# Cross-attention: one accumulated output projection per batch instead of one per step

## The reference, cut to what matters

```python
o = jnp.einsum('bhnm,bhmd->bhnd', a, v)           # a: softmax over 1601 keys
o = o.transpose(0, 2, 1, 3).reshape(xq.shape[0], xq.shape[1], MID)   # MID = 16 * 64
return o @ wo + bo                                # then added to x
```

## Time and profile before

| | us |
|---|---|
| median of 3 runs | 2189.35 (2186.43 to 2197.72) |
| the profiled execution | 2197.43 |
| its span in the trace | 2195.6 |
| PE busy | 2070.3 (94%) |
| DVE busy | 1646.5 (75%) |
| POOL busy | 1169.5 (53%) |
| ACT busy | 998.3 (45%) |
| mean granted TensorE clock | 0.97 of 2.4 GHz |

### The profile page before, as it was taken

One profiled execution on the slowest core, in us unless ns is written; L12 is line 12 of the kernel. 1 busy time (PEld: TensorE's weight loads), 2 busy tenths in 40 slices (PEclk: granted clock), 3 DMA queues, 4 the chain that ended last, 5 costly groups with the idle time before them and its releaser, 6 DMA issues.

```text
span 2195.6 us, 47792 instructions
## 1 busy us (share of the span) xinstructions
PE 2070.3 (94%) x17744; PEld 1412.6 (64%) x17744; DVE 1646.5 (75%) x2426; ACT 998.3 (45%) x1606; POOL 1169.5 (53%) x721
## 2 busy tenths in 40 slices
PE   5888888888699999999999999999999999999988
PEld 3666666622267777777777677777777777777763
DVE  3888888746567877877877787787788778778732
ACT  2444444434244454444444445444444444544433
POOL 1344444300056666666666666666666666666660
PEclk7999999979689999999999999999999999999999
DMA  3522222100111111111111111111111111111100
GB/s 107 161 77 76 76 77 77 53 0 1 41 45 55 49 52 52 52 52 48 52 53 48 55 48 52 52 52 52 48 52 51 49 55 48 52 51 50 51 14 21
DMA packets 109728, 118.32 MB, mean 54 GB/s; under 512 B 18241, under 2 KB 99265, under 8 KB 109249
## 3 DMA queue, kind: packets, MB, share of 16 engines
q1 hardware_dynamic: 109504, 115.27, 15.9%
HBM read 36.52 MB, written 1.05 MB: 17 GB/s over the span
## 4 chain that ended last, share of the span: by engine, by line
PE 89%; DVE 3%; ACT 3%; DMA 3%; issue 2%; SPq 1%; POOL 0%; POOLq 0%; ACTq 0%; DVEq 0%
PE S L1071 20%; PE OB L1083 17%; PE PB L1022 9%; PE PB L1031 9%; PE S L1044 6%; PE S L967 3%; PE OB L977 2%; PE S L879 2%; PE PB L952 2%; PE PB L934 2%; PE PB L1014 2%; PE PB L925 2%; DMA swapped<-turned 2%; PE PB L1092 2%; PE PB L994 1%
## 5 line engine op out<-in xcount | busy, mean ns | idle before, releaser
L502 POOL TENSOR_TENSOR psum_acc<-psum_acc,P 124x1024 f32<-124x1024 f32 (+1 forms) x320 | 688.0, 2150 | 179.8 <-ACT P L627 169.7
L810 DVE TENSOR_REDUCE mxc<-S 128x2 f32<-128x800 f32 (+1 forms) x512 | 507.6, 991 | 230.4 <-PE S L1044 224.9
L627 ACT ACTIVATE P<-S 124x1024 f32<-124x1024 f32 (+1 forms) x448 | 431.4, 963 | 368.3 <-PE S L1071 366.6
L1083 PE MATMUL OB<-P,V 124*64 124x256 f32 (+1 forms) x3328 | 425.7, 387 | 0.0
L495 POOL TENSOR_TENSOR psum_acc<-P 124x1024 f32<-124x1024 f32 x64 | 152.8, 2387 | 348.3 <-ACT P L627 348.3
L519 ACT ACTIVATE V<-PB 124x512 f32<-124x512 f32 (+1 forms) x320 | 157.3, 492 | 330.4 <-PE PB L1031 266.0
L1083 PEld LDWEIGHTS OB<-P,V 124*64 124x64 f32 (+1 forms) x3328 | 220.4, 137 | 115.0 <-issue 15.0
L1071 PE MATMUL S<-QH,KH 64*124 64x256 f32 (+1 forms) x1664 | 268.3, 318 | 4.6 <-ACT P L627 4.6
L1031 PEld LDWEIGHTS PB<-kv_w,ctxT_all 96*124 96x124 f32 (+1 forms) x1664 | 212.3, 188 | 64.0 <-issue 33.0
L1022 PE MATMUL PB<-ctxT_all,kv_w 96*128 96x400 f32 (+1 forms) x512 | 241.4, 554 | 10.9 <-DVE KL L802 7.0
L1031 PE MATMUL PB<-kv_w,ctxT_all 96*124 96x128 f32 (+1 forms) x1664 | 238.8, 282 | 0.1
(11 more groups left out here) (117 smaller groups left out, 3146.7 us busy)
## 6 DMA issues: line engine op xcount, KB each, us to landing
swapped<-turned SPq DMA_DIRECT2D x384, 100.0 KB, 2.0
swapped<-turned SPq DMA_DIRECT2D x128, 128.0 KB, 2.0
swapped<-turned SPq DMA_DIRECT2D x128, 100.2 KB, 2.0
kv_w<-sa_kv_dram SPq DMA_DIRECT2D x64, 128.0 KB, 2.3
qswapped<-qturned SPq DMA_DIRECT2D x128, 64.0 KB, 1.9
kv_w<-ca_kv_dram SPq DMA_DIRECT2D x64, 96.0 KB, 2.2
ctxT_all<-ctxT_dram SPq DMA_DIRECT2D x8, 600.4 KB, 5.1
q_w<-sa_wq_dram SPq DMA_DIRECT2D x64, 64.0 KB, 2.0
```

Of the source, the lines that this page charges most:

```text
L502: pool.tensor_tensor(acc, acc, P_of(J, c)[0:rows, :, 0:w], ALU.add).then_inc(x.acc, 1)
L627: act.activation(P_of(J, c)[0:rows, :, 0:w], SP[0:rows, :, 0:w], ACT.Exp, scale=SCALE).then_inc(x.e, 1)
L810: dve.tensor_reduce(mxc[:, t, :, c:c + 1], MP[:, :, 0:a_.chunks[c][1]], AX.X, ALU.max).then_inc(x.am, 1)
L1083: ins = pe.matmul(OB[half(h), 0:N], Vb[J % 2][0:w, t, half(h)], P_of(J, c)[0:w, h, k * N:(k + 1) * N], start=(t == 0), stop=(t == len(a_.t ...
```

## The change

In steps 0 to 6 of a batch PE no longer projects and DVE no longer adds. `dv` writes the scaled output of each step to its own buffer `oTs[J % 8]` (the eight buffers exist already, for self-attention). In step 7, at the same place of the PE string, eight matmuls add up in `XB`, and DVE adds the sum to `xT` once. The cross-attention's output weights are loaded all eight at once, before the SP queue waits for the end of LNX, and the word `wo` leaves SP's string.

```diff
-                  "w+2 k1+1 q+1 k2+1 wo k3+1 k0+2")
+                  "w+2 k1+1 q+1 k2+1 k3+1 k0+2")
...
-            def cross_out_weights(J, pair):
-                r = J % UNROLL
-                wait(sp, x.y, times(J, 1) - UNROLL + 1)
-                sp.dma_start(o_w[r][:, :], packs["ca"][2][pair]).then_inc(x.wo[r], 16)
...
             sp.wait_ge(LN2.done, NLN)
+            for pair in range(PAIRS):
+                sp.dma_start(o_w[pair][:, :], packs["ca"][2][pair]).then_inc(x.wo, 16)
             sp.wait_ge(LNX.done, NCL)
...
-                    wait(dve, x.y, times(J, 1))
-                    dve.tensor_tensor(oT[:, :], oraw[:, :], XB[:, 0:N], ALU.mult).then_inc(x.ot, 1)
+                    wait(dve, x.y, batch(J))
+                    dve.tensor_tensor(oTs[J % PAIRS][:, :], oraw[:, :], XB[:, 0:N], ALU.mult).then_inc(x.ot, 1)
 
                 def add(J, _):
-                    wait(dve, x.y, times(J, 1) + 1)
-                    wait(dve, x.added, times(J, 1))
-                    x_b = xT[:, batch(J) * N:batch(J) * N + N]
-                    dve.tensor_tensor(x_b, x_b, XB[:, 0:N], ALU.add).then_inc(x.added, 1)
+                    if J % PAIRS == PAIRS - 1:
+                        wait(dve, x.y, batch(J) + 1)
+                        x_b = xT[:, batch(J) * N:batch(J) * N + N]
+                        dve.tensor_tensor(x_b, x_b, XB[:, 0:N], ALU.add).then_inc(x.added, 1)
...
-                           "o": (x.added, lambda K, k: K + 1)}
+                           "o": (x.added, lambda K, k: batch(K) + 1 if K % PAIRS == PAIRS - 1 else None)}
...
                 def output(J, _):
-                    r = J % UNROLL
-                    wait(pe, x.wo[r], J // UNROLL * 16 + 16)
-                    wait(pe, x.ot, times(J, 1) + 1)
-                    x_free(a_, readers, J, ("o", 0))
-                    pe.matmul(XB[:, 0:N], o_w[r][:, :], oT[:, :], start=True, stop=True).then_inc(x.y, 1)
+                    if J % PAIRS == PAIRS - 1:
+                        wait(pe, x.wo, 16 * PAIRS)
+                        wait(pe, x.ot, J + 1)
+                        x_free(a_, readers, J, ("o", 0))
+                        for p in range(PAIRS):
+                            ins = pe.matmul(XB[:, 0:N], o_w[p][:, :], oTs[p][:, :], start=(p == 0),
+                                            stop=(p == PAIRS - 1))
+                        ins.then_inc(x.y, 1)
```

More of the change, by code:

```diff
@@ L138, in block_kernel @@
         oraw = sb("oraw", [PAIR, N])
-        oT = sb("oT", [PAIR, N])
         oraws = [sb(f"oraws{i}", [PAIR, N]) for i in range(2)]
@@ L227, in __init__ @@
                 self.w = [sem(f"{n}_weights_loaded{i}") for i in range(UNROLL)]
-                self.wo = [sem(f"{n}_wo_loaded{i}") for i in range(UNROLL)]
+                self.wo = sem(n + "_wo_loaded")
                 self.qp = sem(n + "_q_projected")
@@ L418, in cross_weights_of @@
                 cross_weights(J, J % PAIRS)
-            def cross_out_weights_of(J, _):
-                cross_out_weights(J, J % PAIRS)
             sp.wait_ge(z.added, B)
             sp.wait_ge(LN2.done, NLN)
+            for pair in range(PAIRS):
+                sp.dma_start(o_w[pair][:, :], packs["ca"][2][pair]).then_inc(x.wo, 16)
             sp.wait_ge(LNX.done, NCL)
-            run_steps(a_, in_order(a_.sp, {"q": swap_q, "k": swap_k, "w": cross_weights_of,
-                                              "wo": cross_out_weights_of}))
+            run_steps(a_, in_order(a_.sp, {"q": swap_q, "k": swap_k, "w": cross_weights_of}))
             sp.wait_ge(x.pv, NU * STEPS)
@@ L837, in cross @@
                     "am": reduce_max, "nm": maximum, "rc": invert, "dv": divide, "ad": add}))
-                dve.wait_ge(x.added, STEPS)
+                dve.wait_ge(x.added, B)
             dve.wait_ge(s_const, 16 * 6)
@@ L1105, in cross @@
                     "m": max_rows, "s": scores, "p": products, "sum": sums, "o": output}))
-                pe.wait_ge(x.added, STEPS)
+                pe.wait_ge(x.added, B)
             pe.wait_ge(s_const, 16 * 6)
```

## The result

The changed kernel takes 2206.07 us (median of 10 runs, 2198.62 to 2208.35) against 2197.47 us (median of 10, 2186.43 to 2200.96) before: ratio 1.0041, 95% interval 1.0025 to 1.0057, so 9.0 us slower, 5.5 to 12.5. The forecast was +13.4 us, and 2202.7 us in all. The two profiled executions differ by as much: spans 2205.2 and 2195.6 us, +9.6 us.

The account below looks back on a forecast made before the run. The prediction took PE's instruction list to bound the kernel: 11.3 us saved and 24.7 us added made +13.4 us on a median of 2189.35, so 2202.7 us, range 2191 to 2214.

Parts of the forecast that it names:

- PE's list sets the time; DVE's additions and SP's loads are hidden: Cross-attention: matmuls taken off or put on PE change the time; DVE's 56 removed additions and SP's moved loads count 0 us.
- A removed output gives the slack behind e1, 0.21 us, and not its 0.44: Before s2 on PE: s2 then waits for ACT's exponential, so 54 places save 0.21 us each, 11.3 us.
- A burst costs 3.09 us: Each batch's last step: seven more output matmuls in a row on PE add 3.09 us, 24.7 us in eight batches.
- The tail: Last batch, end of the chain: 0.68 us of PE grows by 3.09, plus 0 to 1.7 us for a lower clock.
- DVE's easing: Cross-attention: fewer additions and loads between the swaps may shrink DVE's DMA waits that reach PE, gaining 0 to 2.6 us.
- The sum: Whole kernel: 11.3 us saved and 24.7 added give +13.4 us, the tail's clock and DVE's easing taken to cancel.
- the wait does not arise: Rival, before s2: each removed output gives its whole 0.44 us, 24.6 in all, so not slower, 2189.4 us; chance 0.13.
- nothing saved: Rival, shorter rounds: a maximum or swap DMA binds instead, the 11.3 us vanish, 2214.1 us; chance 0.10.
- PE is not the bound: Rival, from the weight loads' share: removed and added matmuls are hidden apart from the tail's 3.1 us, 2192.4 us; chance 0.04.
- The clock: Rival, mid-stage: stops of 0.23 us in each round lower PE's clock, 24 us more, 2226.8 us; chance 0.03.

Follow-up runs that it names:

- e1: Changed kernel with seven of the eight output matmuls in each batch's last step left out; ratio 0.992 to the kernel before, 17.5 us faster.
- e2: Kernel before with the output matmul of each batch's last step done eight times over; ratio 1.0097 to the kernel before, 21.3 us slower.
- e3: Kernel before with all eight output weight loads moved ahead of cross-attention, as in the change; ratio 1.0001 to the kernel before.
- e4: Kernel before with DVE adding only the last pair's output of each batch, PE still projecting all eight; ratio 1.0004 to the kernel before.
- e10: Kernel before with weights loaded ahead and only the last pair's output of each batch added, PE's matmuls unchanged; ratio 1.0001 to the kernel before.
- e8: Changed kernel with query projection q moved on PE from behind p1 to between k1 and s2; ratio 0.9987 to the kernel before, median 2190.66 us.
- e5: Changed kernel with products p0 moved ahead of s2 on PE; ratio 1.0025 to the kernel before.
- e7: Changed kernel with key chunk k1 moved from before s2 to behind it on PE; ratio 1.0346 to the kernel before, 76 us slower.
- e9: Kernel before with query projection q moved on PE from behind p1 to between o and s2; ratio 1.1106 to the kernel before, 243 us slower.
- e6: Kernel before with products p0 moved ahead of s2 on PE; ratio 1.0031 to the kernel before.

## Why the prediction was right

- *PE's list sets the time; DVE's additions and SP's loads are hidden.* Shown by `e1` and `e2`, where matmuls taken off and put on moved the time by −17.5 and +21.3 us, and by `e3`, `e4` and `e10`, three times no change (ratios of 1.0001 to 1.0004, intervals of at most 0.2%).
- *A removed output gives the slack behind e1, 0.21 us, and not its 0.44.* Shown: rounds shorter by 0.22, 54 new waits in just the steps counted, and in `e1` the same without the burst. The handover of 0.145 us, read from a place of the trace before where `k1` was missing, held in all of them (0.143 to 0.146 us). One reading was loose: the single wait of rows 3 is not one of the 60 steps between but that of rows 6 itself; none of the 60 had one.
- *A burst costs 3.09 us.* It cost 3.02 in mid-stage: the 0.2207 us a record were from self-attention, and at this place it was 0.216. Over seven bursts 0.5 us. DVE's wait for it was 1.27 us, where 1.4 or more was forecast; nothing hung on it.
- *The tail: 3.09 us, and 0 to 1.7 for the clock.* 3.71 instead of 0.68 us, without the clock's share; in `e8` that share came, 1.7 us. The burst is the same code in both, so which of the two a run gets is not decided by it: it took 3.71 us in `e2`, `e5` and `e7` as well.
- *DVE's easing −2.6 to 0.* It came, −2.2 us in the profiled execution, though by none of the causes that I named for it.
- The sum was 3.8 us high in the profiled execution (13.4 against 9.6): 2.2 late swaps, 0.5 bursts, 0.6 rounds, 0.5 behind the last burst. I had set the easing off against a loss at the tail that did not come.
- That 2202.7 us came within 3.4 us of the measured 2206.07 is in part luck: ten runs put the kernel before at 2197.47 us, 8.1 above the three-run median that the forecast started from, and the step was 4.4 us too large by the timed runs. The two errors point opposite ways.
- The rivals: *the wait does not arise* fell with the 54 waits; *nothing saved* with `e1`; *PE is not the bound* with `e1` and `e2`, which moved the time by 17 and 21 us, at a share of the weight loads of 282 in 400 us. *The clock* did not fall by stops of 0.22 us (1.00 in both mid-stage stretches above), but `e9` shows where it does: stops of 2.26 us in each round.
- The page of the Trainium skill that this last rival leans on, "Perfetto Trace Analysis", says it in its section "Identifying the Most-Contended Engine", not in the one that the prediction names, and says it of how close a kernel is to the roofline. What bounds this kernel is decided by the measurements of `e1` and `e2`.
- A step that the prediction lacked, since the change did not need it: what a matmul costs depends on its neighbours. It upset the sizes of `e5`, `e6` and `e7` and made `e8`.

## What to carry to other kernels

Work on the engine that is the bound can still be cover for something else: before moving an instruction, subtract it from the place it leaves and ask whether the next one there was about to wait; only the slack is won, the whole length is paid where it goes. Look for a place in the trace before where a neighbour is missing for another reason, as at the end of a loop; it shows the shortest handover without an experiment. When a wait is to be filled, try a matmul of the same kind as its neighbour first: here that paid, and splitting a group did not. And when stretches of two traces are compared, look at the granted clock at their ends before calling a microsecond a gain.

## What the runs showed of the hardware

- What a matmul costs from start to start depends on its neighbours: `q` took 0.63 us between products and scores, where a matmul of the same shape took 0.43 to 0.44 in a row of its kind (two records of 0.216 us in the burst, of 0.2207 in self-attention); sixteen products took 1.88 us as one group and 2.03 us as two; `k1` took 1.06 us between two groups of scores (`e7`), and 0.78 from its start to that of `o` behind it.
- From the end of an exponential on ACT to the first score on PE that waited for it there were 0.143 to 0.146 us, in each of 54 waits of the changed kernel and of `e1`.
- Stops of PE of 0.22 us in every round of 23.6 us, and of 1.02 us in one of 24.7 (`e7`), left the clock at 1.00 from 1000 to 1400 us; with stops of 2.26 us in one of 27.8 (`e9`) its mean there was 0.93, so in part of the stretch it was at 1.2 GHz.
